# Moving attention's four sums in VectorE's order, second layer, middle tiles

## The reference, cut to what matters

```python
xn = _layernorm(x)
x = x + _L1_attn_ref(xn, ...) + _L1_ffn_ref(xn, ...)

# attention, among the 4 sequences at one position: l, m = 0..3, m <= l, 16 heads of 16
attn = softmax(where(causal, einsum('lnhd,mnhd->nhlm', q, k), -inf))
out = einsum('nhlm,mnhd->lnhd', attn, v)          # then @ weight_out.T

# feed-forward, 1024 hidden, 2 of every 4 neighbours kept by magnitude
h = silu(x @ w_gate) * (x @ w_up)
y = _sparsify_2to4(h) @ w_down
```

## Time and profile before

| | |
|---|---|
| time, median of 3 runs (least to most) | 780.61 us (778.89 to 781.29) |
| the profiled execution's own time | 779.57 us |
| its span, first to last instruction | 777.8 us |
| busy: TensorE, VectorE, ScalarE, GpSimd | 92%, 67%, 48%, 17% of the span |
| mean granted TensorE clock | 0.973 of full speed |
| second layer's tiles | from about 577 us to the end |

### The profile page before, as it was taken

One profiled execution on the slowest core, in us unless ns is written; L12 is line 12 of the kernel. 1 busy time (PEld: TensorE's weight loads), 2 busy tenths in 40 slices (PEclk: granted clock), 3 DMA queues, 4 the chain that ended last, 5 costly groups with the idle time before them and its releaser, 6 DMA issues. The chain is left out here.

```text
span 777.8 us, 10577 instructions
## 1 busy us (share of the span) xinstructions
PE 714.2 (92%) x4014; PEld 596.5 (77%) x4014; DVE 520.7 (67%) x940; ACT 376.2 (48%) x783; POOL 135.7 (17%) x121
## 2 busy tenths in 40 slices
PE   2889999969999999999999999998889999999957
PEld 1668888748878788887888878886667888877847
DVE  4635565974776457665676555757558978889776
ACT  4757766654654334443254442446455354553431
POOL 5023454420000001000100001000122202213340
PEclk9979999979999999999999999999989999999979
DMA  4056442100000000000000000220000000000000
GB/s 175 1 161 249 136 122 76 56 1 1 1 1 0 1 1 1 1 1 0 1 1 1 1 1 0 94 125 1 0 1 1 1 27 1 24 4 2 28 0 28
DMA packets 21282, 25.78 MB, mean 33 GB/s; under 512 B 976, under 2 KB 19408, under 8 KB 20464
## 3 DMA queue, kind: packets, MB, share of 16 engines
q1 hardware_dynamic: 20576, 23.79, 9.0%
q10 hardware_dynamic: 656, 1.31, 0.4%
HBM read 22.94 MB, written 2.16 MB: 32 GB/s over the span
## 5 line engine op out<-in xcount | busy, mean ns | idle before, releaser
L1113 DVE TENSOR_TENSOR h_raw<-h_s,bank 128x512 f32<-128x512 f32 x104 | 71.4, 687 | 131.0 <-ACT h_s L1103 115.0
L1103 ACT ACTIVATE h_s<-bank 128x512 f32<-128x512 f32 x104 | 62.0, 597 | 175.5 <-PE bank L91 175.4
L1118 DVE TENSOR_TENSOR h_ring_lo<-h_raw,h_ring_hi 128x512 fp32r<-128x512 f32 x104 | 77.0, 740 | 0.1
L1107 ACT ACTIVATE h_ring_hi<-h_raw 128x512 fp32r<-128x512 f32 x104 | 64.7, 622 | 0.7 <-DVE h_raw L1113 0.7
L89 PE MATMUL bank<-l_xT_hi,l_wgu 128*128 128x512 f32 x128 | 54.1, 423 | 10.0 <-DVE l_h L2269 9.8
L90 PE MATMUL bank<-fused_lo,h_ring_hi 128*128 128x256 f32 (+1 forms) x224 | 62.7, 280 | 0.0
L89 PE MATMUL bank<-f_yT_hi,mlp_hi 128*128 128x512 f32 x128 | 52.5, 410 | 3.0 <-DVEq L1555 3.0
L91 PE MATMUL bank<-l_xT_hi,l_lo 128*128 128x512 f32 x128 | 52.2, 407 | 0.0
L90 PE MATMUL bank<-l_xT_lo,l_wgu 128*128 128x512 f32 x128 | 52.1, 407 | 0.0
L2030 ACT ACTIVATE l_s<-bank 128x512 f32<-128x512 f32 x32 | 19.1, 597 | 68.2 <-PE bank L91 68.1
L91 PE MATMUL bank<-f_yT_hi,fused_lo 128*128 128x512 f32 x128 | 50.8, 397 | 0.0
(11 more groups left out here) (338 smaller groups left out, 2043.3 us busy)
## 6 DMA issues: line engine op xcount, KB each, us to landing
m_W<-m_scratch SPq DMA_DIRECT2D x16, 512.0 KB, 5.9
fused_raw<-in_fused SPq DMA_DIRECT2D x1, 3584.0 KB, 15.4
res<-in_x SPq DMA_DIRECT2D x4, 512.0 KB, 6.1
fused_raw<-in_fused SPq DMA_DIRECT2D x2, 1024.0 KB, 8.3
l_raw<-in_layer SPq DMA_DIRECT2D x1, 2048.0 KB, 8.7
out_x<-res SPq DMA_DIRECT2D x16, 128.0 KB, 1.8
l_raw<-in_layer SPq DMA_DIRECT2D x1, 1280.0 KB, 12.5
fused_raw<-in_fused SPq DMA_DIRECT2D x1, 1152.0 KB, 5.2
```

The source lines that it names most:

```text
L1103: self.nc.scalar.activation(self.s[u % 2][r, :], gate[r, :], ACT.Silu).then_inc(self.silu.sem, 1)
L1107: self.nc.scalar.activation(self.unit(i, u)[0], self.product(i, u), ACT.Copy).then_inc(self.hi.sem, 1)
L1113: self.nc.vector.tensor_tensor(out=self.product(i, u), in0=self.s[u % 2][r, :], in1=up[r, :], op=ALU.mult).then_inc(self.hidden.sem, 1)
L1118: self.nc.vector.tensor_tensor(out=lo, in0=self.product(i, u), in1=f32(hi), op=ALU.subtract).then_inc(self.lo.sem, 1)
```

## The change

In VectorE's `body`, for the three tiles that have a following one, the four calls of `attended` no longer stand together behind the last `keep` of the first half. Sums 0 and 1 are called between `times(i, 4)` and `vote(i, 0)`, sum 2 between `low_x(following)` and `times(i, 6)`, and sum 3 stays where the four were. No instruction and no semaphore is added or taken away, and no other engine's order is changed.

```diff
                 times(i, 3)
                 compare(i, 0)
                 times(i, 4)
+                if following is not None:
+                    attended(i, 0)
+                    attended(i, 1)
                 vote(i, 0)
                 times(i, 5)
                 if following is not None:
                     low_x(following)
+                    attended(i, 2)
                 times(i, 6)
                 keep(i, 0, 0)
                 keep(i, 0, 1)
...
                 keep(i, 0, 2)
                 keep(i, 0, 3)
                 if following is not None:
-                    for l in range(L):
-                        attended(i, l)
+                    attended(i, 3)
                 for j in range(GP):
                     low(i, 0, j)
```

## The result

The changed kernel takes **786.78 us** in the median (786.20 to 787.74, 4 runs) against 780.55 us for the kernel before on the same chip (4 runs): a ratio of 1.010, with a 95% interval of 1.0079 to 1.0122. The change makes the kernel slower by 6.2 us, and the interval does not reach 1. The profiled execution took 786.2 us, with a span of 784.4 us, where the one before had 777.8.

What follows compares the result with a forecast made beforehand. TensorE was taken as nearly the bound of the second layer's tiles. 779.57 + 3.3 (tiles at full clock) + 6.3 (clock falls) = 789.2 us, stated as 789.5 us against the runs' median; range 782 to 795.

Steps and rivals of the forecast that it cites:

- steps 2 and 3: First-half votes of each middle tile stand still behind GpSimd's products 2 and 3; unit 7 starts 3.55 us later.
- steps 4 and 5: Behind unit 7: VectorE's idle waits (1.85 us) go, and TensorE's stalls of 0.95, 1.04 and 0.2 us go.
- step 6: Three middle tiles at full clock, unit 7's delay less regained stalls: some +1.3, +1.0, +1.0 us, together +3.3 us.
- step 7: Clock falls ahead of or in unit 7 of each middle tile: 2.1 us a tile, +6.3 us, bounds 3.6 to 8.6.
- A: Rival in the middle tiles: votes stand still but the clock stays up; 783 us, slower by 0.4%; chance 0.14.
- B: Rival: GpSimd's products don't block the votes, unit 7 only 0.95 us later; -1.25 us a tile, 775.9 us; chance 0.12.
- C: Rival: votes blocked 1.2 us of 2.6, unit 7 2.2 us late, all regained; 779 to 781 us; chance 0.08.
- D: Rival: clock falls last longer than in the last tile and bring more stalls; over 795 us; chance 0.04.

Runs made afterwards that it cites:

- doubled product: Changed kernel with GpSimd's fourth product computed twice in each middle tile: 791.54 us, 3.9 us over the changed kernel on the same chip.
- filled kernel: Changed kernel with 12 useless matmuls ahead of unit 7's wait in each middle tile: 781.41 us on the first chip, 781.37 us on the second.
- later order: Kernel before with sums 0 and 1 moved behind `times(i, 5)` and sum 2 behind `times(i, 6)`: 771.46 us, ratio 0.9907.
- gated kernel: Changed kernel with GpSimd's third product also waiting for the four votes, so no GpSimd work runs beside them: 772.48 us, ratio 0.991.

## Why the prediction was right, point by point

**The block (steps 2 and 3)** was right in mechanism and nearly in every number. Forecast for the second tile: product 2 starts 0.49 us after the first sum, the votes end 6.1 us after it, a stall of 3.7 us as records count it. Measured: 0.49 (639.49 to 639.98), 6.12 (639.49 to 645.61), 3.68. The four votes took 5.17 us where 5.2 were worked out. The experiment with the wait shows that this is the cause, and the doubled product that a third product blocks a third vote. The forecast let the second tile stand for all three; in the first the block is the same, but the stall was 2.94 us.

**Sums 2 and 3 and what lies behind (steps 4 and 5)** were right: both stalls are gone, and moving sum 2 showed no effect. A detail was off: sum 3 starts at 654.31, not before 651.9, since VectorE's `times(i, 7)` waits 2.27 us for the silu of unit 7, which was made at half clock. TensorE's later work covers it. The fourth sum took 2.03 us with GpSimd idle (GpSimd had been idle from 643.8 on), as before beside a GpSimd product: so its length, out of line with the 1.03 of the third, is its own and no contention.

**The sum at full clock (step 6)** was too high: +3.3 us forecast. The filled kernel gives +2.7 us on one chip and +1.3 on the other; by the profiles it is 2.0 to 2.2 over the three tiles, and 0.5 a tile in the second and third where 1.0 was put down. The filled kernel's second tile on the first chip tells the two sides apart. Unit 7 starts 18.36 us after the tile's `add` (626.63 to 644.99), in the kernel before 15.36 (627.18 to 642.54): +3.00, and not +3.55. From there to the next `add` it is 32.42 against 34.85 us: -2.43, and not -2.19. So the term that was mis-sized most is the delay of unit 7. It left out a stall ahead of unit 6 that stood in the kernel before, where a tile's rows are

```profile
634.92 3.84 DVE L2297 TENSOR_TENSOR l_ge<-l_ab 128x1536 bf16<-128x1536 f32 x3 [0.70 <-ACT l_ab L2036]
639.41 0.50 PE L89 MATMUL bank<-l_xT_hi,l_wgu 128*128 128x512 f32 x1 [0.47 <-DVE l_h L2269]
```

and in the changed kernel

```profile
635.48 3.50 DVE L2297 TENSOR_TENSOR l_ge<-l_ab 128x1536 bf16<-128x1536 f32 x3 [0.70 <-ACT l_ab L2036]
639.62 0.50 PE L89 MATMUL bank<-l_xT_hi,l_wgu 128*128 128x512 f32 x1
```

From unit 2's first matmul (626.98 before, 627.79 in the changed kernel) to unit 6's it was 12.43 us, and is 11.83: the 0.6 us of the stall are regained, because `times(i, 4)` comes 0.6 us earlier against TensorE. Of that, 0.25 us are VectorE's lead: `compare` starts 7.69 us after unit 2 in place of 7.94. The other 0.34 are `compare` itself. It starts when GpSimd's products 0 and 1 are all but over (633.91 + 1.65 = 635.56), where it met them before (until 635.40), so it takes 3.50 us and not 3.84. The later order shows the same from the other side: there `compare` takes 3.85 us and the stall stays. The prediction named "a few tenths elsewhere" and let VectorE's lead die out instead of spending it there. In the gated kernel the head of the tile is 0.6 us shorter than expected too (unit 7 comes 15.70 us after `add`, +0.34 and not +0.95); the remaining 0.2 us of its extra gain lie behind unit 7, and are not resolved.

**The clock (step 7)** was right in what happened: three falls, one behind each new stall. The sum, +6.3 us, is also what lies between the changed kernel and the filled one on the second chip, but to the tenth that is luck: the three tiles account for 5.3 to 5.7 us, by single falls 1.3 to 1.6, 2.5 to 2.6 and 1.5, where 2.1 was taken for each, a middle between bounds. The argument was weaker than it looked, too. It said that the new stalls are longer than the two it had looked at. The first tile's stall of 2.94 us is shorter than the 3.32 us that the step leaned on, and the clock fell behind it as well. In the kernel before, a wait of 2.37 us, shorter than the 2.60 us after which the clock stayed up, has the clock at 1.2 GHz behind it (0.50 from 756.6 to 759.9):

```profile
756.37 0.35 PE L89 MATMUL bank<-l_wd,l_ring_hi 128*128 128x256 f32 x1 [2.37 <-DVE l_ring_lo L2316]
```

And one and the same wait goes either way. Ahead of unit 3 of the first tile, where the change has touched nothing yet, TensorE waits 2.83 us in both kernels. In the profiled execution of the kernel before the clock fell in it, in that of the changed kernel it did not (granted clock 1.00 from 574.8 to 577.5). In the changed kernel's execution on the second chip (2.84 us) it fell again. The two matmuls behind the wait, the kernel before first:

```profile
576.39 0.79 PE L89 MATMUL bank<-l_xT_hi,l_wgu 128*128 128x512 f32 x1 [2.83 <-DVE l_h L2269]
574.83 0.50 PE L89 MATMUL bank<-l_xT_hi,l_wgu 128*128 128x512 f32 x1 [2.83 <-DVE l_h L2269]
```

So the length of a stall alone doesn't decide it, and for the first tile's 2.94 us the fall was likely by these cases, not sure. What else decides was not tested. The same stall followed by half clock in one execution and not in the next is also one source of the spread between executions outside of the edited parts.

**The total.** A rise of 9.6 us was added up; the first comparison had 6.2, the second chip 7.6 (1.3 and 6.3 us by the two terms). In the first comparison's profiled executions the three tiles rise by 7.5 us. So some 2 us of the 3.4 too many are these tiles', rather more of them step 6's than step 7's, and the rest is time outside of them, 0.9 us shorter in the changed kernel's execution, and spread between runs. The 789.5 us that were stated are only 2.7 too high, since 9.6 us on top of the median (780.61) would have been 790.2; that is luck, too.

**The rivals.** A (the clock stays up) is out by the stretches at 0.50. B (no block) is what the gated kernel was made to do, at 772.5 us and not 775.9, mostly for the reason just given. C and D are out: the votes took the full 5.17 us, and the falls lasted no longer than the 5.7 us of matmuls of the one in the last tile (the longest, in the second tile, from 646.35 to 652.06).

## What to carry to other kernels

When a step is moved ahead, look at what its signal lets go on the other engines, and at what then runs beside that: here the two sums ahead of the votes cost 0.95 us, and the GpSimd products that they set free cost 2.6 us more by stopping VectorE instructions with two SBUF inputs. Let GpSimd's work fall beside VectorE's reads of PSUM and its reductions, if need be with a wait of its own: the same order went from +1.0% to -0.9% by that. And price a stall of TensorE with its echo: behind 3.7 us of waiting, another 1.5 to 2.6 us were lost to half clock, and filling the stall with matmuls of no use bought that back. But don't take one trace's falls of the clock for fixed: the same 2.83 us of waiting had one in one execution and none in the next.

## What the runs showed of the hardware that was not expected

GpSimd can be kept out by VectorE for very long. In the kernel with the later order the product of scores for l = 0 (256 elements, 0.74 us in the kernel before) took 6.22 us:

```profile
648.34 6.22 POOL L2161 TENSOR_TENSOR l_prod<-l_q,l_k 128x256 f32<-128x256 f32 x1 [5.11 <-ACT l_k L2083]
```

It began while VectorE worked on the first `low`, and behind that stood six more VectorE instructions with two inputs in SBUF, three `low` and three comparisons, none of which had to wait:

```profile
648.07 2.48 DVE L2316 TENSOR_TENSOR l_ring_lo<-l_h,l_ring_hi 128x512 fp32r<-128x512 f32 x4
...
653.28 0.68 DVE L2297 TENSOR_TENSOR l_ge<-l_ab 128x512 bf16<-128x512 f32 x1
```

The four `low` and three comparisons kept their full pace (2.48 us for four), and the product ended at 654.56, behind the end of the comparisons at 653.96. One tile later, in the same execution, it went the other way: the two products of scores took 2.69 us together and `low` lost 1.6 us.

```profile
695.99 4.11 DVE L2316 TENSOR_TENSOR l_ring_lo<-l_h,l_ring_hi 128x512 fp32r<-128x512 f32 x4
696.27 2.69 POOL L2161 TENSOR_TENSOR l_prod<-l_q,l_k 128x256 f32<-128x256 f32 x2 [5.11 <-ACT l_k L2083]
```

In all three tiles of the changed kernel it also went this way (4.13 or 4.14 us for four `low`), and between the first two votes GpSimd got in as well. What decides whether the waiting engine gets its turn between two VectorE instructions is open. A pause in VectorE's queue is not it: in the third tile the second `low` starts 0.60 us after the first (695.99 to 696.59), as in the second tile (648.07 to 648.67), and GpSimd's product starts 0.27 and 0.28 us after the first `low`. So which of the two a tile gets can't be read from these rows, and a forecast should carry up to 1.6 us of it as a range.
